# Six patch chunks of 128 rows, delay bits computed beside the embedding, delays and first projections on 128 + 64 rows

## The reference

```python
# patches: 64 images x 16 patches, 768 values each -> 1024 tokens of 192
h = patches @ W + b + pos_emb[token % 16]          # (1024, 768) @ (768, 192)
# level 0 attention, on sequences of 16 tokens
s = layernorm(h)                                   # the "spikes"
# one delay of 1 to 15 for each of the 192 features:
# d[b, t, e] = s[b, t - delay[e], e], or 0 where t < delay[e]
q, k, v = d @ Wq, d @ Wk, d @ Wv                   # 192 x 192 each
k = k * 192 ** -0.5 + 0.1 * clip(decay * membrane + 0.01 * mean(q), -2, 2)
h = h + softmax(mask(q @ k.T)) @ v @ Wo + bo
```

## Time and profile before

| what | value |
|---|---|
| time, median of 3 runs | 1658.72 us (1656.53 to 1665.37) |
| the profiled execution's own time | 1651.06 us, its span 1649.3 us |
| granted clock of PE, mean over the span | 0.90 |
| busy: PE, PEld, DVE, ACT, POOL | 85%, 65%, 38%, 29%, 31% |
| embedding | from the start to 33.02 us |
| norm, up to the first instruction of the delay bits | 33.02 to 41.51 us |
| delay bits | 41.51 to 49.62 us |
| delays | 49.62 to 68.78 us |
| first projections | 68.78 to 92.91 us |

### The profile page before, as it was taken

One profiled execution on the slowest core, in us unless ns is written; L12 is line 12 of the kernel. 1 busy time (PEld: TensorE's weight loads), 2 busy tenths in 40 slices (PEclk: granted clock), 3 DMA queues, 4 the chain that ended last, 5 costly groups with the idle time before them and its releaser, 6 DMA issues. The chain is left out here.

```text
span 1649.3 us, 35913 instructions
## 1 busy us (share of the span) xinstructions
PE 1406.3 (85%) x14614; PEld 1076.0 (65%) x14614; DVE 630.8 (38%) x1654; ACT 478.9 (29%) x1278; POOL 504.6 (31%) x650
## 2 busy tenths in 40 slices
PE   7387856999999999599999999858759995886997
PEld 6164334788885899488887589724539994362756
DVE  2544764433334322233333512155441113453434
ACT  0430151434342121244344212124213332421121
POOL 0010274323221365322232236423126662320000
PEclk9697966999999999799999999979659997977999
DMA  5000202000000642300000254210034552010000
GB/s 132 0 30 14 86 7 89 5 2 2 9 12 11 227 135 93 130 3 2 2 9 15 96 179 133 99 51 5 28 131 128 189 186 88 4 60 1 30 29 19
DMA packets 40279, 101.86 MB, mean 62 GB/s; under 512 B 15920, under 2 KB 26292, under 8 KB 34992
## 3 DMA queue, kind: packets, MB, share of 16 engines
q0 software_dynamic: 18480, 58.56, 10.3%
q1 hardware_dynamic: 19904, 38.62, 7.2%
q10 hardware_dynamic: 1728, 2.36, 0.5%
HBM read 138.06 MB, written 11.50 MB: 91 GB/s over the span
## 5 line engine op out<-in xcount | busy, mean ns | idle before, releaser
L206 PE MATMUL bank<-blk,ident 128*128 128x384 f32 x140 | 76.1, 686 | 80.3 <-PEq L179 62.4
L206 PEld LDWEIGHTS bank<-blk,ident 128*128 128x128 f32 x140 | 34.5, 266 | 105.4 <-issue 103.0
L1283 PE MATMUL bank<-t_ew,t_hg 128*128 128x192 f32 x552 | 97.2, 327 | 0.0
L1283 PEld LDWEIGHTS bank<-t_ew,t_hg 128*128 128x128 f32 x552 | 88.7, 190 | 0.2
L1315 ACT ACTIVATE t_hg<-bank 128x384 f32<-128x384 f32 x92 | 40.1, 488 | 166.9 <-PE bank L1271 166.9
L1538 DVE SCALAR_TENSOR_TENSOR h<-bank,cw,h 128x192 f32<-128x192 f32 x128 | 53.5, 418 | 88.6 <-PE bank L1461 71.8
L1311 ACT ACTIVATE l_hg<-bank,l_ew 128x128 f32<-128x128 f32 x186 | 51.3, 375 | 99.6 <-PE bank L1271 99.6
L2117 POOL TENSOR_SCALAR t_rstd<-t_ssq 128x1 f32<-128x1 f32 x64 | 12.2, 190 | 218.8 <-ACT t_junk L1953 218.7
L1267 PE MATMUL bank<-t_xgT,t_ew 128*128 128x128 f32 x552 | 71.5, 281 | 2.8 <-DVE t_xgT L1347 2.8
L1175 POOL DMA_INDIRECT t_ew<-in_t_moe,source x46 | 47.5, 1032 | 79.8 <-DVE t_og L1356 52.0
L1874 PE MATMUL bank<-t_wo,t_ctx 128*128 128x192 f32 x384 | 71.0, 335 | 0.9 <-ACT t_ctx L1970 0.9
(11 more groups left out here) (362 smaller groups left out, 3061.5 us busy)
## 6 DMA issues: line engine op xcount, KB each, us to landing
t_qkv<-in_t_wqkv SPq DMA_DIRECT2D x9, 576.0 KB
t_wo<-in_t_wo SPq DMA_DIRECT2D x8, 576.0 KB
w<-in_l_w SPq DMA_DIRECT2D x8, 576.0 KB, 4.2
wA<-in_t_wqkv SPq DMA_DIRECT2D x2, 1728.0 KB
patches<-in_patches SPq DMA_DIRECT2D x8, 384.0 KB, 9.2
rows_in<-rows SPq DMA_DIRECT2D x24, 128.0 KB, 1.7
t_wi<-in_t_wi SPq DMA_DIRECT2D x3, 576.0 KB
t_gg<-rows_out ACTq DMA_DIRECT2D x8, 192.0 KB, 4.3
```

Of the source, the lines that this page charges most:

```text
L206: pe.matmul(bank[:, 0:HPU * P], k.ident[:], k.blk[:].rearrange("p j q -> p (j q)"), start=True, stop=True)
L1283: mm = pe.matmul(k.bank[6 + b % 2][:, 0:DIM], k.hg[b % 2][:, m, :], w[:, SPLIT + m * DIM:SPLIT + (m + 1) * DIM], start=(m == 0), stop=(m = ...
```

## The change

Patches stand as 6 chunks of 128 rows. Three small loads (`pos`, the bias, `delays`) are issued behind the first patch tile, five constants before the last two tiles, and sixteen loads move to SP's queue in the norm, which becomes a phase of its own (`spikes_phase`). The delay bits move to DVE's list in the embedding, the zeros to POOL's. The features are split as 128 + 64: `xe[0]` has 128 rows and 64 sequences, `xe[1]` has features 128 to 191 of sequences 0 to 31 on rows 0 to 63 and of sequences 32 to 63 on rows 64 to 127. Delays and projections follow that split. The phase of the delay bits goes.

```diff
-PATCH_CHUNKS = 8
+PATCH_CHUNKS = 6
...
-def embed_phase(k, patches, w, pos, tri01, consts, loads, sources):
+def embed_phase(k, patches, w, pos, tri01, delays, early, consts, sources):
...
             for t in range(NT):
+                if t == 1:
+                    for dst, src in early:
+                        sp.dma_start(dst, src).then_inc(k.w_loaded[1], 16)
+                if t == NT - 2:
+                    for dst, src in consts:
+                        sp.dma_start(dst, src).then_inc(k.loaded, 16)
                 sp.dma_start(patches[:, t], sources[1][t]).then_inc(k.row_in[t], 16)
-            for dst, src in consts:
-                sp.dma_start(dst, src).then_inc(k.loaded, 16)
-            issue_loads(sp, k, loads, len(consts))
+            sp.wait_ge(k.loaded, 16 * len(consts))
+
+        @block.gpsimd
+        def _(pool):
+            for xe in k.xe:
+                pool.memset(xe[:, :, 0:SEQ], 0.0)
...
-            dve.wait_ge(k.loaded, 16 * (len(consts) + len(loads)))
+            dve.wait_ge(k.w_loaded[1], 16 * len(early))
             link(dve.tensor_tensor(pos[:], pos[:], k.bias[:], ALU.add))
...
+            s = k.shift
+            link(dve.tensor_copy(s[:], delays[:]))
...
+            for i, step in enumerate((16, 8, 4, 2, 1)):
+                link(dve.tensor_scalar(k.bit[:, i, :], s[:], float(step), None, ALU.is_ge))
+                link(dve.scalar_tensor_tensor(s[:], k.bit[:, i, :], -float(step), s[:], ALU.mult, ALU.add))
+                dve.tensor_scalar(k.nbit[:, i, :], k.bit[:, i, :], -1.0, 1.0, ALU.mult, ALU.add)
...
             for t in range(NT):
+                if t == NT - 1:
+                    dve.wait_ge(k.loaded, 16 * len(consts))
+                    for j in range(HPU):
+                        dve.tensor_scalar(k.maskb[:, j, :], k.blk[:, j, :], -1.0, BIG, ALU.add, ALU.mult)
...
                 dve.wait_ge(k.turned, t + 1)
                 dve.tensor_tensor(k.h[:, t, :], k.bank[t][:, 0:DIM], pos[:], ALU.add)
...
+def spikes_phase(k, loads):
...
+    first, other = [k.bank[0][:], k.bank[1][:]], k.bank[2][:]
+    half = BATCH // 2
...
+            issue_loads(sp, k, loads)
...
+        def _(act):
+            act.wait_ge(k.std_in, 1)
+            act.activation(k.std[:], k.var[:], ACT.Sqrt).then_inc(k.std_out, 1)
+            for n in range(2):
+                act.wait_ge(k.turned, 4 * (n + 1))
+                act.activation(k.xe[0][:, n * half:(n + 1) * half, SEQ:2 * SEQ], seqs(first[n]), ACT.Copy)
+                act.activation(k.xe[0][:, n * half:(n + 1) * half, 2 * SEQ:3 * SEQ],
+                               seqs(first[n])[:, :, SEQ - 1:SEQ].broadcast_to([P, half, SEQ]), ACT.Copy)
...
+            dve.wait_ge(k.turned, NT)
+            dve.tensor_copy(k.xe[1][:, :, SEQ:2 * SEQ], seqs(other))
+            dve.tensor_copy(k.xe[1][:, :, 2 * SEQ:3 * SEQ],
+                            seqs(other)[:, :, SEQ - 1:SEQ].broadcast_to([P, half, SEQ]))
...
+            idle_products(pe, k, k.bank[7], 4)
+            for t in range(NT):
+                n, cols = t // 4, slice(t % 4 * P, (t % 4 + 1) * P)
+                pe.wait_ge(k.normed, t + 1)
+                pe.transpose(first[n][:, cols], k.xn[:, t, 0:P], k.ident[:])
+                pe.matmul(other[n * REST:(n + 1) * REST, cols], k.xn[:, t, P:DIM], k.ident[:], start=True,
+                          stop=True).then_inc(k.turned, 1)
...
-                    act.activation(k.moved[:, c, :, 0:widths[i]],
-                                   k.xe[:, c, :, steps[i]:steps[i] + widths[i]], ACT.Copy,
+                    act.activation(k.moved[c][:, :, 0:widths[i]],
+                                   k.xe[c][:, :, steps[i]:steps[i] + widths[i]], ACT.Copy,
                                    scale=k.bit[:, i, c:c + 1]).then_inc(k.evacuated_a, 1)
...
-            for i, (which, m, n) in enumerate(jobs):
-                for c in range(2):
-                    mm = pe.matmul(k.bank[i][0:CH, :], w[:, which, c, m * CH:(m + 1) * CH],
-                                   dT[:, c, n * HALF:(n + 1) * HALF], start=(c == 0), stop=(c == 1))
-                mm.then_inc(k.turned, 1)
...
+            for i in range(0, len(jobs), 2):
...
+                for n in range(2):
+                    pe.matmul(k.bank[i + n][0:CH, :], w[:, which, 0, cols], dT[0][:, n * HALF:(n + 1) * HALF],
+                              start=True, stop=False)
+                for n in range(2):
+                    pe.matmul(k.bank[i + n][0:CH, :], w[halves[n], which, 1, cols], dT[1][halves[n], :],
+                              start=False, stop=True).then_inc(k.turned, 1)
+            for t in range(NT // 2):
+                pe.wait_ge(k.evacuated_a, NT // 2 + t + 1)
+                for n in range(2):
+                    tok = (4 * n + t) * P
+                    pe.matmul(k.bank[4 * n + t][:, 0:DIM], dT[0][:, tok:tok + P], w[:, 2, 0, :], start=True, stop=False)
+                for n in range(2):
+                    pe.matmul(k.bank[4 * n + t][:, 0:DIM], dT[1][halves[n], t * P:(t + 1) * P], w[halves[n], 2, 1, :],
+                              start=False, stop=True).then_inc(k.turned, 1)
...
+            for t in range(NT // 2):
+                for n in range(2):
+                    dve.wait_ge(k.turned, len(jobs) + 2 * t + n + 1)
+                    dve.tensor_copy(v[:, 4 * n + t, :], k.bank[4 * n + t][:, 0:DIM])
...
+                spikes_phase(k, [(w0, a["l0_w"]), (woA, a["l0_wo"]), (k.bias[:], a["l0_bo"]), (k.scal[:], a["scal"]),
+                                 (k.feat[:], a["feat"]), (k.wrs[:, :, 0:8], a["l0_wr"]), (k.rb[:, 0:8], a["l0_rb"]),
+                                 (k.headmask[:], a["headmask"]), (k.rope[:], a["rope"]), (k.before[0][:], a["before8"]),
+                                 (k.before[1][:], a["before16"]), (k.before[2][:], a["before16p"]),
+                                 (k.home[:], a["home"]), (k.part[:], a["part"]), (k.cont[0][:], a["cont8"]),
+                                 (k.cont[1][:], a["cont16"])])
```

More of the change, by code:

```diff
@@ L783, in rope_projection_phase, with seqs @@
     end_phase(k)
[L788 to L801, removed]
-            for c in range(2):
[L804 to L813, removed]
+def spikes_phase(k, loads):
+    def seqs(ap):
+        return ap.rearrange("p (b s) -> p b s", s=SEQ)
+    first, other = [k.bank[0][:], k.bank[1][:]], k.bank[2][:]
+    half = BATCH // 2
     with k.nc.Block(no_gpsimd_drain=True) as block:
@@ L844, in l0_projection_phase @@
     jobs = [(which, m, n) for which in range(2) for m in range(2) for n in range(2)]
+    halves = [slice(o * REST, (o + 1) * REST) for o in range(2)]
     with k.nc.Block(no_gpsimd_drain=True) as block:
@@ L847, in _ @@
         def _(pe):
-            for i, (which, m, n) in enumerate(jobs):
-                for c in range(2):
-                    mm = pe.matmul(k.bank[i][0:CH, :], w[:, which, c, m * CH:(m + 1) * CH],
-                                   dT[:, c, n * HALF:(n + 1) * HALF], start=(c == 0), stop=(c == 1))
-                mm.then_inc(k.turned, 1)
[L853 to L858, removed]
+            for i in range(0, len(jobs), 2):
+                which, m, _n = jobs[i]
+                cols = slice(m * CH, (m + 1) * CH)
+                for n in range(2):
[12 more added lines that the diff above has]
+                              start=False, stop=True).then_inc(k.turned, 1)
         @block.scalar
@@ L2247, in build @@
         wrope = k.wA[:, 0:8 * DIM]
[L2248 removed]
+        w0 = k.wA[:, 0:3 * 2 * DIM].rearrange("p (w c n) -> p w c n", w=3, c=2)
         woA = k.wA[0:CH, 5 * 2 * DIM:6 * 2 * DIM].rearrange("p (c n) -> p c n", c=2)
@@ L2260, in build @@
         with stage() as st:
[L2261 to L2277, removed]
-            with stage() as sub:
[L2279 to L2288, removed]
+            dT = [tensor(st, "dT0", [P, TOK]), tensor(st, "dT1", [P, HALF])]
@@ new lines, in build @@
+            with stage() as sub:
+                k.xe = [tensor(sub, f"xe{c}", [P, n, 3 * SEQ]) for c, n in enumerate((BATCH, BATCH // 2))]
+                k.shift = tensor(sub, "shift", [P, 2])
+                k.bit = tensor(sub, "bit", [P, 5, 2])
+                k.nbit = tensor(sub, "nbit", [P, 5, 2])
+                with stage() as first:
+                    patches = tensor(first, "patches", [P, NT, PATCH_CHUNKS, P])
+                    wtok = tensor(first, "wtok", [P, PATCH_CHUNKS, DIM])
+                    pos = tensor(first, "pos", [P, DIM])
+                    tri01 = tensor(first, "tri01", [P, P])
+                    delays = tensor(first, "delays", [P, 2], I32)
+                    embed_phase(k, patches, wtok, pos, tri01, delays,
+                                [(pos[:], a["pos"]), (k.bias[:], a["btok"]), (delays[:], a["delays"])],
+                                [(k.ident[:], a["ident"]), (k.blk[:], a["blk"]), (k.near[:], a["near"]),
+                                 (tri01[:], a["tri"]), (k.iota[:], a["iota"])], (a["wtok"], a["patches"]))
```

(18 more changed lines are left out.)

36 lines of the change are left out of this document (24 added, 12 removed).

## The result

The changed kernel's median is 1637.86 us (1629.8 to 1646.48, 8 runs), that of the kernel before 1656.22 (1647.69 to 1665.37, 8 runs). The ratio is 0.9898 with a 95% interval of 0.9869 to 0.9928, so 12 to 22 us were saved, 17 by the ratio. The prediction said 14.5, and 1644.2 with a range from 1637 to 1652. It reckoned from 1658.72 us, the median of three runs, and the eight runs of the kernel before have a median 2.5 us lower. The measured time is 0.9 us above the bottom of the range and outside the forecast's own 1641 to 1648. The profiled execution took 1635.77 us, its span 1633.9.

What follows compares the result with a forecast made beforehand. PE was taken to bound embedding and projections, DVE to lead norm, bits and delays. Savings of 5.6 + 5.8 + 1.4 + 1.7 = 14.5 us take the median from 1658.72 to 1644.2 us, range 1637 to 1652.

Steps and rivals of the forecast that it cites:

- signs that the prediction had named for being wrong: SP's issues over 0.5 us, PE over 0.7 us a tile in the norm, or clock 0.50 beyond 7 us of work.
- Embedding: First phase: 96 passes in 18.9 us against 24.1 save 5.2, an earlier start 0.4; together 5.6 us.
- The earlier start: Embedding: weights and first tile load faster in 128 rows, gaining between 0 and 1.2 us; 0.4 taken.
- The covers: Embedding: loads, DVE's bits and casts, and POOL's zeros all lie under PE's work; bits uncovered would cost some 4 us.
- Norm and bits: Second phase: 16.6 us become 10.8, between SP's loads at 10.5 and PE with copies at 11.0; 5.8 saved, bounds 6.1 and 2.0.
- PE's stream: Norm: a transposition and a two-pass product take 0.55 us a tile, done at T + 8.5; bounds T + 6.5 and 10.5.
- Delays: Delay phase: 18.0 us become 16.6, so 1.4 saved; bounds 0 and 3.6.
- The chain through c = 0: Delays: ACT's c = 0 rounds wait for DVE's previous round; 7.29 + 8.12, some 0.5 and 0.74 make 16.6 us.
- Projections: Four groups of 2.92 plus 3.2 give 14.9 us against 16.9; net 1.7 saved, bounds minus 1.7 and plus 3.1.
- the costlier change of shape: Rival: norm lasts 13.0 us, 2.2 lost, and 3.4 more if 64-row pairs run in turn; 1646.4 to 1649.8 us, 12%.
- The loads' 0.73 us: Rival: SP's loads take 0.73 us each, norm lasts 14.6 us, total saving 10.7, time 1648.0 us; 13%.
- The slow clock over the projections: Rival: PE's clock does not rise in the projections, and PE work up to 112 us doubles; + 29, 1673 us, 3%.

Runs made afterwards that it cites:

- e6: Changed kernel with the patches again as 8 chunks of 96 rows, all else kept: embedding 34.0 us, PE's start at 7.0 us.
- e5: Kernel before, without an edit, profiled a second time: embedding 34.3 us, norm 8.4, bits 8.1, delays 19.2, attention and output projection together 21.4.
- e2: Changed kernel with the sixteen loads moved from the norm to the delays' phase: norm 13.8 us, delays 17.7 us.
- e3: Changed kernel with transpositions alone in the norm, ACT copying the last 64 features beside them in place of the 64-column product: norm 11.0 us.
- e4: Changed kernel with both the edits of e2 and e3 (loads under the delays, transpositions alone in the norm): norm 9.8 us, delays 17.7 us.
- e8: Changed kernel with the delays in three units of 32 sequences instead of units of 64 and 32: delays 15.0 us, 2.6 less.
- e11: Changed kernel with the q and k products in two groups instead of four: projections 21.0 us against 21.7.
- e10: Changed kernel with transpositions alone, loads under the delays, delays in thirds, 16 idle PE products: median 1626.62 us, ratio to the kernel before 0.9846.

## Why the prediction was right

Direction and size held, and the range held narrowly, but not because each term did: 2.5 us that the embedding gave beyond its term stand against 2.3 that the norm fell short, and that the two cancel is luck. Two of the signs that the prediction had named for being wrong did come, both in the norm: PE needed over 0.7 us a tile once its clock had fallen, and SP's sixteen issues took 8.07 us, a hair over 0.5 each. In its own order:

- **Embedding, 5.6 predicted, 8.1 measured** (mean of two profiles of before, 33.6, and of the ten with chunks of 128, 25.5). The 32 passes are 5.2, as said. The earlier start was mis-sized: 0.4 was taken, "near the first, since the same descriptor pattern is nearer", and e6 shows 1.25 (6.98 against 5.73), just over the upper bound. The third part, 1.7, was not foreseen: the prediction kept 20 slow passes on both sides. With chunks of 96 there were 20, 30 and 28 (before, e5, e6), with chunks of 128 between 9 and 18, mean 15. The covers held: DVE's bits were done at 10.3 and its last tile waited for PE, not for a load.
- **Norm and bits, 5.8 predicted, 3.5 measured** (16.6 less the mean of seven, 13.1). The estimate for PE's stream, 0.55 us a tile, was 0.62. The step that failed is the assumption beside it, never written down, that the clock would stay up through the norm. A smaller slip stands in the sum: of two things the later ends the phase, so 10.5 and 11.0 give 11.0 and not 10.8. At full clock the phase is 11.7 against 10.8 predicted; with the fall 13.7, above the 13.0 that was the bound. That the loads would be as long as the work was wrong at either clock: they end at 9.6 us, PE and the copies at 10.4 or 12.4, and taking the loads away gave nothing (e2); with PE mended they do bound the phase (e3, e4).
- **Delays, 1.4 predicted, 1.5 measured.** The chain through c = 0 gives it and e8 confirms it by taking the chain away; DVE's busy time alone would have said 3.6.
- **Projections, 1.7 predicted, 2.2 measured** (means 23.7 and 21.5). Groups of 2.92, pairs of v of 1.37, copies of k and v without a new wait: all as worked out. The rest is the draw of the clock's rise. The 64-row products run together, four records in 1.10 us, and a change of shape costs 0.16 us in e11, little beside the full product that each pair saves. The Trainium skill (TensorEngine Tiling (Array Packing), Tiling Modes) says that tiles work in parallel and that a change of mode drains TensorE. This case agrees with both by these numbers, though no run shows that the 0.16 us are the drain.
- **Behind it, nothing predicted.** Attention and output projection took 19.7 and 21.4 us before and 21.3 to 24.4 in ten of the eleven profiles after: 1.6 more on average, with the clock at its lower level for some us in each that took longer. Two profiles of before are too few to say whether that comes with the change. In e10, where PE had been busy under the delays, they took 19.7.

Together these phases give 8.1 + 3.5 + 1.5 + 2.2 - 1.6 = 13.7 us, within the measured 12 to 22 and below its middle of 17. The other 3 us, if they are real, stand behind the output projection, in code that is the same: from there to the end it is 1536.7 and 1541.5 us in the two profiles of before (mean 1539.1), and 1532.6 to 1540.9 in the eleven after (mean 1536.1). The profiles of each side differ among themselves by more than the means do, so no cause can be named. Of the rivals, the costlier change of shape came nearest, in the norm alone, and by the clock: 0.62 us a tile lies under its 0.81, and 1.02 above. The loads' 0.73 us did not return (0.50 each on average); read rightly, it would have been 0.79, since 13 loads and not 14 stand from 8.99 to 19.26. The slow clock over the projections did not come.

## What to carry to other kernels

When two engines hand work to and fro, making one of two equal units shorter can turn a pipeline into a chain: count the round trip of the longest unit, not the busy time, and cut all units alike (17.7 to 15.0 us here). A term made of many short PE instructions should be priced at both levels of the clock, and a stage in which PE idles, as the delays, can carry a few idle products that give the next one its clock back (21.6 to 19.1 us), if they are counted to end before it. When a wait is taken away, look for the next one close behind: moving the loads gained nothing (e2) and then 1.3 us (e4), depending on what stood with them.

## What the runs showed that was not expected

- **Rows and the clock's rise.** From PE's first pass of the embedding, with no pause in either case, the clock rose after 6.6, 9.7 and 9.1 us with operands of 96 rows, and after 3.0 to 6.0 us in all ten profiles with 128. The two do not overlap. The 9.1 is e6, where the chunks alone were put back, so the late rise goes with them; but that is one profile, the rows in use, the number of passes and the loads changed together, and the cause is open. In the projections, 96 rows before and 128 + 64 after, it rose after 6.4 and 4.5 us and after 3.1 to 5.6, which do overlap.
- **Rows and the loads.** The same 3.7 MB of patches and weights moved at some 269 GB/s in rows of 4096 bytes on 96 partitions and at 360 in rows of 3072 on 128, by the window of the changed kernel's first us of work:

```profile
5.70:12.00 6.30, 6.27 (x21) 6.30 (x22) 3.38 (x22) 0.00 (x0) 0.00 (x0) 1.00 1.02 360
```

The DMA share is 1.02 and 1.03, so the DMA engines are busy throughout in both. Whether the partitions or the row length make the difference was not tried. The row also shows the clock column at 1.00 where PE makes 21 passes in 6.3 us, most of them of 0.326 us, the lower level: at the start of an execution, until the clock's first rise, the column can't be trusted.
